# The value products of an attention unit, sent in two parts of two heads instead of one block of four

## The reference

```python
HIDDEN, HEADS = 128, 16
q = (x @ Wq.T + bq).reshape(b, s, HEADS, HEAD_DIM)
k = (x @ Wk.T + bk).reshape(b, s, HEADS, HEAD_DIM)
v = (x @ Wv.T + bv).reshape(b, s, HEADS, HEAD_DIM)
attn = jnp.einsum('bqhd,bkhd->bhqk', q, k) / np.sqrt(HEAD_DIM)
attn = jax.nn.softmax(attn, axis=-1) * head_mask[None, :, None, None]
out = jnp.einsum('bhqk,bkhd->bqhd', attn, v).reshape(b, s, HIDDEN)
return out @ Wo.T + bo
```

## Time and profile before

| what | value |
|---|---|
| time, median of 3 runs | 2099.72 us |
| the profiled execution's own time | 2100.33 us |
| its span | 2098.1 us |
| TensorE busy | 1860.1 us, 89% |
| VectorE busy | 1496.2 us, 71% |
| ScalarE busy | 1232.2 us, 59% |
| GpSimd busy | 887.4 us, 42% |
| mean granted TensorE clock | 0.929 of full speed |

### The profile page before, as it was taken

How to read it: one execution, slowest core, us unless ns; L and a number is a source line. 1 busy time by engine, 2 the same in 40 slices (tenths; PEclk the granted TensorE clock), 3 DMA queues, 4 the chain that set the end, 5 groups by cost and what they waited for, 6 DMA issues and landing times. The chain is left out here.

```text
span 2098.1 us, 30450 instructions
## 1 busy us (share of the span) xinstructions
PE 1860.1 (89%) x9600; PEld 1108.9 (53%) x9600; DVE 1496.2 (71%) x2379; ACT 1232.2 (59%) x1914; POOL 887.4 (42%) x875
## 2 busy tenths in 40 slices
PE   3999999999937898999999988888859999999999
PEld 2777777777812333333333333333247777777777
DVE  4767777687517878777787777887447768776775
ACT  3566455555513767666676667776635565556654
POOL 2566555655621222222222222221125565556655
PEclk9999999999955989888888889998879999999999
DMA  2000000000032323222223223222010000000000
GB/s 91 21 11 31 27 24 30 10 30 10 16 59 33 47 47 47 47 42 39 41 44 44 41 41 40 53 44 35 12 36 21 31 11 31 20 30 10 30 14 16
DMA packets 43167, 68.57 MB, mean 33 GB/s; under 512 B 9916, under 2 KB 11444, under 8 KB 43060
## 3 DMA queue, kind: packets, MB, share of 16 engines
q1 hardware_dynamic: 38256, 65.15, 15.7%
q0 software_dynamic: 4096, 1.08, 0.3%
q10 hardware_dynamic: 708, 0.98, 0.1%
HBM read 28.36 MB, written 12.58 MB: 20 GB/s over the span
## 5 line engine op out<-in xcount | busy, mean ns | idle before, releaser
L1259 DVE TENSOR_REDUCE attn_neg_max<-attn_p_score 128x2 f32<-128x1024 f32 x512 | 624.8, 1223 | 211.2 <-PE attn_p_score L941 209.1
L572 POOL TENSOR_TENSOR ffn_hid_low<-ffn_hidden,ffn_hid_high 128x512 fp32r<-128x512 f32 x448 | 580.6, 1298 | 454.9 <-ACT ffn_hid_high L512 454.2
L1096 ACT ACTIVATE attn_exps<-attn_p_score 128x1024 f32<-128x1024 f32 x512 | 519.8, 1025 | 286.6 <-PE attn_p_score L927 284.6
L512 ACT ACTIVATE ffn_hid_high<-ffn_hidden 128x512 fp32r<-128x512 f32 x448 | 281.0, 627 | 255.7 <-DVE ffn_hidden L705 254.8
L503 ACT ACTIVATE ffn_silu<-ffn_p_gate 128x512 f32<-128x512 f32 x448 | 264.0, 589 | 207.8 <-PE ffn_p_gate L375 207.5
L698 DVE TENSOR_TENSOR ffn_gated<-ffn_silu,ffn_p_up 128x512 f32<-128x512 f32 x352 | 240.6, 684 | 175.1 <-PE ffn_p_up L375 112.2
L941 PE MATMUL attn_p_score<-k_pack,q_pack 24*128 24x512 f32 x1024 | 283.2, 553 | 57.7 <-ACT attn_exps L1096 33.0
L958 PE MATMUL attn_p_o<-attn_exps,values 128*32 128x512 f32 x2048 | 312.0, 684 | 8.4 <-ACT attn_o_raw L1102 3.3
L927 PE MATMUL attn_p_score<-q_pack,k_pack 26*128 26x512 f32 x1024 | 271.2, 539 | 14.9 <-DMA q_pack<-attn_max_rows 14.6
L927 PEld LDWEIGHTS attn_p_score<-q_pack,k_pack 26*128 26x128 f32 x1024 | 101.4, 198 | 314.7 <-issue 207.5
L705 DVE TENSOR_TENSOR ffn_hidden<-ffn_gated,ffn_p_spread 128x512 f32<-128x512 f32 x352 | 241.2, 685 | 14.9 <-PE ffn_p_spread L416 4.1
(11 more groups left out here) (146 smaller groups left out, 2220.9 us busy)
## 6 DMA issues: line engine op xcount, KB each, us to landing
q_pack<-attn_q_high SPq DMA_DIRECT2D x128, 64.0 KB
k_pack<-attn_k_high SPq DMA_DIRECT2D x128, 64.0 KB
ffn_x_in<-in_x SPq DMA_DIRECT2D x16, 256.0 KB, 2.8
ffn_x_res<-in_x SPq DMA_DIRECT2D x16, 256.0 KB, 2.8
after_ffn<-ffn_x_out SPq DMA_DIRECT2D x16, 256.0 KB, 2.0
attn_x_in<-after_ffn SPq DMA_DIRECT2D x16, 256.0 KB, 4.6
k_pack<-attn_k_low SPq DMA_DIRECT2D x64, 64.0 KB
q_pack<-attn_q_low SPq DMA_DIRECT2D x64, 64.0 KB
```

What stands on the lines that cost most here:

```text
L512: nc.scalar.activation(hid_high[s][0:n, :], hidden[s][0:n, :], ACT.Copy).then_inc(high_ready, 1)
L572: nc.gpsimd.tensor_tensor(hid_low[s][0:n, :], hidden[s][0:n, :], hid_high[s][0:n, :].bitcast(F32), ALU.subtract).then_inc(low_ready, 1)
L1096: nc.scalar.activation(exps[n % len(exps)][:], score_bank("exp", b, n)[:], ACT.Exp, scale=inv_sqrt)\
L1259: V.tensor_reduce(neg_max[g % 2][:, j:j + 2, t], score_bank("max", b, n)[:], AX.X, ALU.max, negate=True).then_inc(max_read, 1)
```

## The change

The value products of a unit are sent in two calls, with two heads each: heads 0 and 1 behind the score pairs of the next unit's first half, and ahead of the small job, heads 2 and 3 behind those of its second half. Each call waits only for the exponential that it needs. The wait for `o_copied` moves with the first product, into the first half; `pv_done` is counted behind the second call as before. At the end of the last batch both calls follow each other.

```diff
@@ -944,22 +944,23 @@
                                             tile_position=(j * ROWS, 0))
                 last.then_inc(max_tile, 1)
 
-            def times_values(b, u):
+            def times_values(b, u, half):
 
                 g, t = divmod(u, NT)
-                pe.wait_ge(exp_ready, b.count(PAIRS, 2 * (u + 1)))
-                if t == 0:
+                pe.wait_ge(exp_ready, b.count(PAIRS, 2 * u + half + 1))
+                if t == 0 and half == 0:
                     need(pe, o_copied, b.count(NQ, g))
-                if u == 0:
+                if u == 0 and half == 0:
                     first_batch = isinstance(b.j, int) and b.k == 0
                     pe.wait_ge(x_bank_drained, FIRST_USES.index("v") + 1 if first_batch
                                else uses(b.step(-1), "v") + 1)
-                for h in range(QUAD):
+                for h in (2 * half, 2 * half + 1):
                     last = nc.tensor.matmul(p_o[h * COLS:(h + 1) * COLS, :],
                                             values[b.par][:, t, g * QUAD + h, :],
                                             exps[(2 * u + h // 2) % len(exps)][:, h % 2, :], start=t == 0, stop=t == NT - 1,
                                             tile_position=(0, h * COLS))
-                last.then_inc(pv_done, 1)
+                if half == 1:
+                    last.then_inc(pv_done, 1)
 
             def turn_max(b, g, n):
                 pe.wait_ge(max_split, b.count(MAX_SPLIT * NQ, MAX_SPLIT * (g + 1)))
@@ -1002,12 +1003,12 @@
                         score_exp(b, u, half)
                         if there(ahead):
                             score_max(ahead, v, half)
+                        if u > 0:
+                            times_values(b, u - 1, half)
+                        elif not is_first:
+                            times_values(a, UNITS - 1, half)
                         if half == 0:
                             pieces(b, u, is_first)
-                        elif u > 0:
-                            times_values(b, u - 1)
-                        elif not is_first:
-                            times_values(a, UNITS - 1)
 
             def pieces(b, u, is_first):
                 a, c, e = b.step(-1), b.step(1), b.step(2)
@@ -1056,7 +1057,8 @@
                 if u == NT - 1:
                     turn_max(begin, 0, 7)
             every_batch(pe, batch)
-            times_values(end, UNITS - 1)
+            times_values(end, UNITS - 1, 0)
+            times_values(end, UNITS - 1, 1)
             turn_o(end, NQ - 1, last_uses)
             turn_norm(last_uses + 1)
             project_out(last_uses + 2)
```

## The result

| | before | changed |
|---|---|---|
| median | 2101.63 us (4 runs, 2094.6 to 2109.0) | 2308.69 us (4 runs, 2294.8 to 2312.27) |
| profiled execution | 2100.33 us | 2312.27 us |
| mean granted TensorE clock | 0.929 | 0.936 |

The ratio is 1.097, 95% interval 1.091 to 1.103: the change makes the kernel 207 us slower. Forecast were 2245 us with a range of 2105 to 2400, and 0.87 for slower. Direction and chain held; 64 us of the time were missing. The measured time lies above the forecast's own 2210 to 2300 and nearer to rival 2's 2338; only the wider range, which takes in rivals 1 and 2, holds it.

The account below looks back on a forecast made before the run. A chain between engines, 3.04 us a unit, was taken to bound the attention stage. Terms 775 + 124 + 99 + 17 = 1015 us against 869, +146, gave 2245 us, range 2105 to 2400.

Parts of the forecast that it names:

- chain: Attention stage: waits between TensorE and ScalarE's exponential set the pace, 3.04 us for a unit without small work.
- rival 2: Attention stage: the clock falls as often as now, 22% of the time cold, about 2338 us; chance 0.14.
- rival 1: Value products: half blocks at half cost, 0.57 us each, not slower, 2112 us; chance 0.12.
- The half block at 0.99: Value products on TensorE: two heads take as long as four, 0.99 us more TensorE time per unit.
- 3.04 and the piece, 775 + 124: Attention units: small jobs lose their shadow; 255 steps of 3.04 make 775 us, the small jobs add 124.
- The moved wait at 1.57, 63 times: Units 1, 5, 9, 13: the first half block waits for ScalarE's copy of p_o, +99 us in all.
- The sum at full clock: Attention stage: empty-unit pace, small jobs and copy waits at full clock, 775 + 124 + 99 us.
- I take full clock in the steady part: Attention stage: half blocks fill TensorE's idles of 0.72 us, so the clock is near 1.00, already in the 775.
- the new 1.77 idle four times a batch: TensorE in units waiting for the copy: named as speaking against full clock.
- L958 "near 500 us busy": TensorE's value product groups: sign to look for, near 500 us busy, not 312.
- The loss at the boundary: TensorE between scores and values: 0.20 us lost by changing tiling mode; without the loss there the forecast would be 2160.
- Rival 3: Attention stage: the clock stays down for most of it, half the columns being empty, 2600 to 2900 us; chance 0.12.

Follow-up runs that it names:

- a_twice: The changed kernel with all four heads' products in each of the two calls, so each product is made twice: 2307.25 us, ratio 1.101.
- a_copy: The changed kernel with ScalarE's copy of p_o ahead of the first exponential in units 1, 5, 9 and 13: 2172.78 us, ratio 1.033.
- b_early: The kernel before, with the whole block of four value products moved to behind the first half's scores, ahead of the small job: 2571.67 us, ratio 1.223.
- b_turnfill: The kernel before, with the second quad's maxima turned in unit 0 and unread identity transposes in units 1, 5, 9 and 15: 2078.48 us, ratio 0.994.
- a_both: The changed kernel's split only in units 15 and 0, plus the second quad's maxima turned in unit 0: 2094.89 us, ratio 1.005.
- b_turn: The kernel before, with the second quad's maxima turned and copied in unit 0 instead of unit 1: 2076.61 us, ratio 0.991.
- b_fill: The kernel before, with four unread transposes of the identity in the empty units 15 and 0: 2099.44 us, ratio 0.995.

## Why the prediction was right, and where its size was off

- **The half block at 0.99: right.** It takes 0.98 at full clock; `a_twice` shows it with the order of the calls unchanged. Reading "two records of a head in sequence" off the value projection was enough to reject 0.57.
- **3.04 and the piece, 775 + 124: right,** to 0.02 a unit in the groups of units above, but for unit 14.
- **The moved wait at 1.57, 63 times: right at full clock.** 2.20 behind the scores was forecast and measured. The table's batch at full clock is 62.9; the forecast's was 16 x 3.04 + 8.2 + 6.3 = 63.1.
- **The sum at full clock: right.** 255 steps by the medians of the changed kernel are 16 x 62.94 - 3.03 = 1004, and units at full clock stayed 4 below their medians, so 1000. The forecast's were 775 + 124 + 99 = 998.
- **"I take full clock in the steady part": wrong, and the whole of the error.** For the first units at half clock and ScalarE's copies the sum held 6 us; the clock cost 82. The DMA waits, for which it had 11 more, are already in the 1000. So 998 + 11 + 6 = 1015 stands against 1000 + 82 = 1082: 9 too many on the chain, 76 too few on the clock.

How the clock step failed can be seen in the changed kernel, TensorE in unit 9 of the next batch:

```profile
1090.93 0.50 PE L927 MATMUL attn_p_score<-q_pack,k_pack 26*128 26x512 f32 x2
1091.14 0.50 PE L941 MATMUL attn_p_score<-k_pack,q_pack 24*128 24x512 f32 x2
1093.13 1.05 PE L958 MATMUL attn_p_o<-attn_exps,values 128*32 128x512 f32 x4 [1.49 <-ACT attn_o_raw L1104]
1094.11 0.28 PE L968 MATMUL attn_p_x<-ident,attn_max_parts 128*32 128x128 f32 x1
1094.33 0.80 PE L927 MATMUL attn_p_score<-q_pack,k_pack 26*128 26x512 f32 x2
...
1095.06 1.92 PE L958 MATMUL attn_p_o<-attn_exps,values 128*32 128x512 f32 x4
```

And the stretches before, at and behind the fall:

```profile
1086.00:1094.30 8.30, 6.81 (x37) 2.15 (x37) 5.41 (x5) 4.97 (x6) 0.44 (x2) 1.00 0.00 1
1094.30:1101.20 6.90, 6.90 (x25) 1.97 (x24) 2.45 (x2) 2.71 (x4) 2.41 (x3) 0.51 0.01 2
```

TensorE comes through 8.3 us at 1.00 with 1.49 idle for the copy near their end, and right behind the half block and the turn that follow it is at 1.2 GHz (0.80 for a pair of scores, 1.92 for a half block), with TensorE busy all the while; at 1101.2 it is back. Half clock touches units 1, 5, 9 and 13 in 8, 9, 9 and 11 batches, unit 0, where it was in ten batches before, in one, and unit 15 in none. Of the 37 falls in the stage 36 begin during one of the 63 copy waits or within 2 us behind it. The half blocks did fill the idles of the earlier trace rows, as forecast; the copy waits took their place as the cause. The prediction named them ("the new 1.77 idle four times a batch") and gave them no price in its own sum, only in rival 2. `a_copy` shows the link by experiment: with the wait cut from 1.5 to 0.45 (21.4 us in 48), half clock all but vanishes (18 us).

So two of the prediction's cases came true together. The chain is the forecast's; the clock, 0.91 where 1.00 was forecast, is rival 2's (0.89). Rival 2's own price fits: at half clock a batch takes 104 where it takes 63, a loss of 0.39 per us; 197 us by that are 78, measured are 82. Its full sum, 2338, was too high by 30 mainly because it took 22% at half clock, and it is 18%. Before, half clock was cheaper: a unit without a small job took 4.50 there (654.28 to 658.78 in the trace of before) where it takes 3.04 at full clock, a loss of 0.32 per us, or 66 for its 204 us. A part of the loss passed while TensorE would have waited for the exponential anyway, whose 1.02 does not change with TensorE's clock. The change took that shelter away.

- **L958 "near 500 us busy": 594.8.** 512 x 0.98 is 502, but a half block's records end 0.07 after the next start (1.05 against 0.98), which makes 538; `a_copy`, with hardly any half clock, has 540.1. The other 55 are the same clock step.
- **Rival 1 fell** with `a_twice` and the two-at-a-time rows. Its sum had a slip: by the working of the moved wait a copy's unit would be 2.20 + 0.57 + 0.19 + 1.62 = 4.58 against 2.81, less 0.20, so 1.57 more and not 1.15. That is 26 us, so rival 1 would have been 2139, 1.9% slower, where the recorded text says not slower. The Trainium skill's rule behind it ("TensorE: Matmul & The Clock Gate", Part 3: MATMULs start and end in program order, first in, first out) does not carry the sum here: by it the block's first four records would be two heads and half a block would take half the time, and it takes 0.98 of 1.00. The runs don't tell whether the queue reorders or whether the records are put down head by head at all.
- **The loss at the boundary stayed.** Between scores and half block are 0.43 (1010.99 to 1011.42), as before the change, wherever the half block doesn't wait for a copy. The Trainium skill's "TensorEngine Tiling (Array Packing)", Key Properties, has the rule that a change of tiling mode drains TensorE, and the rows fit it (0.43 against 0.23 between two operand projections). No run here takes the drain away, so the 0.20, and 2160 without it, are differences of rows and not experiments.
- **Rival 3** had its condition, but in `b_early`: 0.60 for the stage. It can't have come from half-used columns, since every block of `b_early` has all four heads; it went with an idle in each unit. The Trainium skill says in "TensorE: Matmul & The Clock Gate", Part 1 (A second HAM failure mode), that frequent short idles between groups of matmuls can make the clock go back and forth; `b_early` agrees: its stage goes to half clock 46 times, with 180.8 us in idles of some 0.7 to 0.9.

**What stays open.** How much of `b_turnfill`'s and `a_both`'s gain the longer DMA wait takes (the profiles show 8 and 6 us of it), and why that DMA comes late for unit 8. Also which idles bring the clock down: 0.72 in each of two units, 1.49 once, and some 0.8 in each unit all went before falls, while `a_copy` with 0.45 in the mean, three times a batch, had next to none.

## What to carry to other kernels

Where small products run side by side on column tiles, look at how many records run at once inside the block: here a block of two heads took 0.98 and one of four 1.00, so splitting it by columns doubled its time. What counts for the pace is then where the parts stand: the second half block lay in an idle and was free, the first one ate the room in which the small jobs lay. When a product is moved earlier in an in-order queue, look at what its first user waits for on the other engine; here one copy, 0.6 us long but queued behind an exponential, was worth 139 of 209 us. And if a wait is shortened, look for the one that takes over: in `a_copy`, `b_turn`, `b_turnfill` and `a_both` it was the same DMA. A clock that follows idles must be priced with the new idles of the changed kernel, in its own term with both ends, even if the old idles are gone.

## What the hardware did that I had not expected

- The clock went with TensorE's idles and not with its records. `b_early` has the records of the kernel before, idles 265 of 1338 us and goes from 0.89 to 0.60; the changed kernel has TensorE held 283 us longer by L958, idles 103 of 1082 and is at 0.91; `a_copy` idles 39 of 943 and is at 0.99.
- Stretches at half clock lasted 3.4 to 6.8 us in the changed kernel's steady part. In the kernel before they were mostly 13.7 to 20.5. About as much time in shorter pieces, 36 of 37 begun in a copy wait or right behind one.
- The granted clock was 0.91 with two heads in a call and 0.92 with four.
- Taking away one cause of a fall moved it to the next (`b_fill`: from units 0 to 3 to units 5 to 12).
